# Ternary feedforward: the second quantisation moved to the middle of a VectorE step, the bias matmuls ahead of its transposes, and one ScalarE eviction between the two activations

## The reference

```python
def act_quant(x):
    scale = 127.0 / jnp.clip(jnp.max(jnp.abs(x), axis=-1, keepdims=True), 1e-05)
    q = jnp.clip(jnp.round(x * scale), -128.0, 127.0) / scale
...
def bitlinear158(x, w, b):
    xq = act_quant(rms_norm(x))
    wq = weight_quant(w)
    return jnp.einsum('bsd,od->bso', xq, wq) + b
...
h = jax.nn.silu(bitlinear158(x, w1, b1))
h = jax.nn.gelu(h, approximate=False)
h = layer_norm(h, ln_g, ln_b)
return bitlinear158(h, w2, b2)
...
x = _layernorm(x + _L1_ffn_ref(x, ...), axis=-1)
```

## Time and profile before

| | us |
|---|---|
| median of 3 runs | 2614.13 |
| lowest and highest | 2604.57, 2614.92 |
| the profiled execution, its own time | 2613.25 |
| its span, first to last instruction | 2611.5 |

### The profile page before, as it was taken

One profiled execution on the slowest core, in us unless ns is written; L12 is line 12 of the kernel. 1 busy time (PEld: TensorE's weight loads), 2 busy tenths in 40 slices (PEclk: granted clock), 3 DMA queues, 4 the chain that ended last, 5 costly groups with the idle time before them and its releaser, 6 DMA issues. The chain is left out here.

```text
span 2611.5 us, 32892 instructions
## 1 busy us (share of the span) xinstructions
PE 1969.5 (75%) x11984; PEld 1450.6 (56%) x11984; DVE 1357.5 (52%) x2704; ACT 741.0 (28%) x1233; POOL 450.7 (17%) x470
## 2 busy tenths in 40 slices
PE   3258888323665999999999995999968996267766
PEld 2135555222434777777877784787846774133333
DVE  8657766486554232222322314566554776456666
ACT  1015555100211221121121112222214002565565
POOL 0122321000000000000000001010103765023334
PEclk9859998656876999999999997999988998588887
DMA  4099995312534000000000003000013114500000
GB/s 177 21 139 153 145 158 85 113 36 83 175 112 162 1 17 18 1 17 18 1 17 17 9 1 113 17 33 17 17 44 137 43 41 152 202 8 25 24 17 24
DMA packets 111911, 169.17 MB, mean 65 GB/s; under 512 B 9104, under 2 KB 65040, under 8 KB 109328
## 3 DMA queue, kind: packets, MB, share of 16 engines
q1 hardware_dynamic: 102672, 150.35, 23.2%
q10 hardware_dynamic: 9088, 16.78, 1.7%
HBM read 120.70 MB, written 46.14 MB: 64 GB/s over the span
## 5 line engine op out<-in xcount | busy, mean ns | idle before, releaser
L1317 DVE TENSOR_TENSOR f_hid<-f_gate,f_gu 128x256 f32<-128x256 f32 x264 | 111.1, 421 | 437.5 <-ACT f_gate L1229 434.3
L1229 ACT ACTIVATE f_gate<-f_gu 128x256 f32<-128x256 f32 x264 | 100.6, 383 | 485.9 <-PE f_gu L1140 352.1
L453 DVE TENSOR_REDUCE a_rowmax<-a_ring 128x2 f32<-128x512 f32 x256 | 165.0, 687 | 100.6 <-PE a_ring L532 98.5
L1974 PE MATMUL e_py<-e_kv,e_toep 128*128 128x320 f32 x640 | 179.1, 435 | 0.0
L1152 PE MATMUL f_gu<-f_low,f_bg 128*128 128x256 f32 x704 | 168.1, 380 | 6.5 <-DVE f_hid L1317 6.5
L1166 PE MATMUL f_pout<-f_wd,f_hid 128*128 128x512 f32 x352 | 165.4, 592 | 0.0
L1140 PE MATMUL f_gu<-f_xhi,f_wg 128*128 128x256 f32 x704 | 152.1, 314 | 4.1 <-issue 4.1
L405 ACT ACTIVATE a_prob<-a_sT 128x1024 f32<-128x1024 f32 x128 | 130.6, 1026 | 81.8 <-PE a_sT L521 81.7
L1974 PEld LDWEIGHTS e_py<-e_kv,e_toep 128*128 128x128 f32 x640 | 119.2, 190 | 45.7
L1152 PEld LDWEIGHTS f_gu<-f_low,f_bg 128*128 128x128 f32 x704 | 127.9, 190 | 28.4 <-issue 10.5
L1140 PE MATMUL f_gu<-f_xhi,f_wu 128*128 128x256 f32 x704 | 133.4, 288 | 0.0
(11 more groups left out here) (348 smaller groups left out, 4416.1 us busy)
## 6 DMA issues: line engine op xcount, KB each, us to landing
a_qs<-parts SPq DMA_DIRECT2D x96, 128.0 KB, 6.6
a_ks<-parts SPq DMA_DIRECT2D x96, 128.0 KB, 7.0
parts<-a_hi SPq DMA_DIRECT2D x16, 512.0 KB, 8.7
parts<-a_lo SPq DMA_DIRECT2D x16, 512.0 KB, 8.7
e_toep<-in_taps SPq DMA_DIRECT2D x32, 256.0 KB
a_xf<-in_xT SPq DMA_DIRECT2D x1, 4096.0 KB, 21.1
ctxT<-a_turned SPq DMA_DIRECT2D x16, 256.0 KB, 9.6
a_cf<-ctxT SPq DMA_DIRECT2D x1, 4096.0 KB, 13.1
```

Source lines behind the costliest of these rows:

```text
L453: dve.tensor_reduce(rowmax[:, s % 2, :, e * SLOTS + j], ring[n % RING][:, :].rearrange("p (q t) -> p q t", t=T), AX.X, ALU.max, negate=Tru ...
L1229: act.activation(gate[:, (u * H + n) % 2, :], gu[f % 4][:, 0, :], ACT.Silu).then_inc(gate_ready, 1)
L1317: dve.tensor_tensor(hid[:, f % 4, j, :], gate[:, (u * H + n) % 2, :], gu[f % 4][:, 1, :], ALU.mult).then_inc(hid_ready, 1)
L1974: last = pe.matmul(py[n % RING][:, 0:DIAG * BS], toep[:, h % 3, (t - j) * P:(t - j + 1) * P], kv[:, h % 2, j, :], start=(j == 0), stop=(j ...
```

## The change

Three orders inside a step change; no instruction is added or taken away, and no shape, buffer or wait changes.

- VectorE: the second quantisation (lag 5) goes from before L2339 to behind the tail's L2349, and the input's largest magnitude (L2353, lag 0) goes from behind the tail to ahead of it.
- TensorE: the bias matmuls (L2264, with their wait for `silu_done`) go from behind the transposes L2253 to ahead of them.
- ScalarE: the eviction `q1f` (L2208) goes from ahead of both activations to between the first and the second.

```diff
@@ -2202,15 +2202,15 @@
                         act.wait_ge(s_["mean_ready"], t + 1)
                         act.activation(junk[:, 0, :], ha[:, t % 3, :], ACT.Square, bias=hs[:, t, 1:2],
                                        accum_out=hs[:, t, 2:3]).then_inc(s_["var1"], 1)
-                    t = tile_at(s, 1)
-                    if t is not None:
-                        act.wait_ge(s_["q1_turned"], t + 1)
-                        act.activation(q1f[:, t % 2, :, :], pq1[:, :].rearrange("p (k t) -> p k t", k=KT), ACT.Identity,
-                                       bias=minus[:, :]).then_inc(s_["q1f_ready"], 1)
-                    for lag in ((2, 3) if s % 2 == 0 else (3, 2)):
+                    for first, lag in ((True, 2), (False, 3)) if s % 2 == 0 else ((True, 3), (False, 2)):
                         t = tile_at(s, lag)
                         if t is not None:
                             silu(t) if lag == 2 else gelu(t)
+                        t = tile_at(s, 1) if first else None
+                        if t is not None:
+                            act.wait_ge(s_["q1_turned"], t + 1)
+                            act.activation(q1f[:, t % 2, :, :], pq1[:, :].rearrange("p (k t) -> p k t", k=KT), ACT.Identity,
+                                           bias=minus[:, :]).then_inc(s_["q1f_ready"], 1)
                     t = tile_at(s, 0)
                     if t is not None:
                         act.wait_ge(got_x[t % XT], 16 * (t // XT + 1))
@@ -2242,6 +2242,16 @@
                         for j in range(KT):
                             last = pe.transpose(pq1[:, j * P:(j + 1) * P], xq[:, t % 2, j * P:(j + 1) * P], keep["ident"][:, :])
                         last.then_inc(s_["q1_turned"], 1)
+                    t = tile_at(s, 1)
+                    if t is not None:
+                        pe.wait_ge(s_["diag_ready"], t + 1)
+                        if t >= 1:
+                            pe.wait_ge(s_["silu_done"], t)
+                        else:
+                            pe.wait_ge(s_["w_ready"], KT)
+                        for n in range(QB):
+                            pe.matmul(p1[:, n * 512:(n + 1) * 512], diag[:, t % 2, :], b1[:, n * 512:(n + 1) * 512],
+                                      start=True, stop=False)
                     t = tile_at(s, 5)
                     if t is not None:
                         pe.wait_ge(s_["q2_ready"], t + 1)
@@ -2255,14 +2265,6 @@
                             last.then_inc(s_["q2_turned"], 1)
                     t = tile_at(s, 1)
                     if t is not None:
-                        pe.wait_ge(s_["diag_ready"], t + 1)
-                        if t >= 1:
-                            pe.wait_ge(s_["silu_done"], t)
-                        else:
-                            pe.wait_ge(s_["w_ready"], KT)
-                        for n in range(QB):
-                            pe.matmul(p1[:, n * 512:(n + 1) * 512], diag[:, t % 2, :], b1[:, n * 512:(n + 1) * 512],
-                                      start=True, stop=False)
                         pe.wait_ge(s_["q1f_ready"], t + 1)
                         for n in range(QB):
                             for j in range(KT):
@@ -2324,13 +2326,6 @@
                         xs.step(dve.tensor_scalar(row[:, 8:9], row[:, 5:6], wfac[:, :], None, ALU.mult))
                         dve.tensor_scalar(diag[:, t % 2, :], keep["ident"][:, :], row[:, 8:9], None, ALU.mult
                                           ).then_inc(s_["diag_ready"], 1)
-                    t = tile_at(s, 5)
-                    if t is not None:
-                        row, y = row2[:, t, :], hc[:, t % 2, :]
-                        dve.wait_ge(s_["root2"], t + 1)
-                        dve.wait_ge(s_["max2"], t + 1)
-                        scales(ys, row, 1)
-                        dve.tensor_scalar(y, y, row[:, 7:8], ROUND, ALU.mult, ALU.add).then_inc(s_["q2_ready"], 1)
                     t = tile_at(s, 4)
                     if t is not None:
                         dve.wait_ge(s_["var1"], t + 1)
@@ -2338,6 +2333,13 @@
                             dve.wait_ge(s_["q2_turned"], (t - 1) * KT)
                         dve.scalar_tensor_tensor(hc[:, t % 2, :], ha[:, t % 3, :], hs[:, t, 1:2], gain[:, :], ALU.add, ALU.mult
                                                  ).then_inc(s_["gained"], 1)
+                    t = tile_at(s, 0)
+                    if t is not None:
+                        dve.wait_ge(got_x[t % XT], 16 * (t // XT + 1))
+                        dve.tensor_reduce(row1[:, t, 3:4], xt[:, t % XT, :], AX.X, ALU.max, apply_absolute_value=True
+                                          ).then_inc(s_["max1"], 1)
+                        if t == 1:
+                            ternary(1)
                     t = tile_at(s, 6)
                     if t is not None:
                         x = xt[:, t % XT, :]
@@ -2347,13 +2349,13 @@
                         dve.wait_ge(s_["added"], t + 1)
                         tails.step(dve.bn_stats(stats[:, t, 0:6], x))
                         dve.bn_aggr(stats[:, t, 6:8], stats[:, t, 0:6]).then_inc(s_["var_ready"], 1)
-                    t = tile_at(s, 0)
+                    t = tile_at(s, 5)
                     if t is not None:
-                        dve.wait_ge(got_x[t % XT], 16 * (t // XT + 1))
-                        dve.tensor_reduce(row1[:, t, 3:4], xt[:, t % XT, :], AX.X, ALU.max, apply_absolute_value=True
-                                          ).then_inc(s_["max1"], 1)
-                        if t == 1:
-                            ternary(1)
+                        row, y = row2[:, t, :], hc[:, t % 2, :]
+                        dve.wait_ge(s_["root2"], t + 1)
+                        dve.wait_ge(s_["max2"], t + 1)
+                        scales(ys, row, 1)
+                        dve.tensor_scalar(y, y, row[:, 7:8], ROUND, ALU.mult, ALU.add).then_inc(s_["q2_ready"], 1)
                     t = tile_at(s, 4)
                     if t is not None:
                         y = hc[:, t % 2, :]
```

## The result

| | before | changed |
|---|---|---|
| median, us (4 runs each) | 2611.04 | 2569.43 |
| lowest, highest | 2604.57, 2614.92 | 2568.12, 2572.93 |
| profiled execution, its span | 2611.5 | 2568.5 |
| last stage in it, first weight load to the end | 395.0 | 361.5 |

The account below looks back on a forecast made before the run. TensorE and ScalarE, waiting for each other in a 20.5 us loop per step, bound the kernel. Terms -42.9, -7.1, -5.1 and +11.7 net -43.4: 2569.9 from the profiled 2613.25, 2570.7 against the median, said 2571; range 2556 to 2588.

Parts of the forecast that it names:

- ten periods: Between the first and eleventh `w2` products: five odd-even pairs of 32.5 us, 162.5 against 205.4, 42.9 less.
- the eleventh: The eleventh period between `w2` products, 20.17 us before, becomes an even step without the magnitude, 13.1: 7.1 less.
- fill: From first `w1` to first `w2` product, 68.4 us before: four first steps together 5.1 shorter, `q1f` no longer delaying the activation.
- The ring: TensorE and ScalarE waiting for each other in a closed chain, 20.5 us a step, VectorE no part; the change opens it.
- An odd step, 18.8 us: Transposes 0.45, TensorE idle 3.95 until SiLU ends, slow-clock bias 5.22, transposes and evictions 2.3, products 6.9.
- The bound I gave above it: Whole odd-step bias at the low clock, 7.0 us instead of 5.22: 8.9 us more in all, kernel 2580.
- An even step, 13.7 us: Bias at full clock; VectorE's second quantisation ends last, transposes begin 4.5 us after `w2`, then 2.3 and 6.9.
- a sign of being wrong: Prediction counts as wrong if TensorE waits for VectorE's rounding in the middle steps too, not only the last four.
- The drain: Last four periods, input tiles gone: moved quantisation uncovered behind the tail; 11.9, 14.4, 14.4, 11.5, together 52.2 against 40.55, 11.7 lost.
- The clock did not hold through the wait: Rival: clock stays up through odd steps' 3.95 us idle; odd steps 17.1, kernel 2562 or less; chance 0.17.
- VectorE did not become the bound of the middle steps: Rival: VectorE and ScalarE bound every step, even steps at 15.0 instead of 13.7; kernel 2580 to 2590; chance 0.14.
- the dearer rivals: VectorE and ScalarE bounding every step (0.14), or TensorE at low clock all odd step, 10.6 more each, 2624 (0.05).

Follow-up runs that it names:

- two second traces: The kernel of before and the changed kernel each traced once more with no edit; last stage 396.2 and 359.8 us.
- x5_fill: Changed kernel plus four f32 matmuls with unused results between the input's transposes and the bias in odd steps; 2561.0 us, ratio to before 0.9803.
- x1_dve_old: Changed kernel with VectorE's order put back to that of before, TensorE and ScalarE keeping the new orders; 2553.7 us, ratio to before 0.978.

## Why the prediction came out right, and where it was off

The forecast of 2571 against 2569.4 is closer than its steps, and that closeness is luck. Against the stage's own rows:

| term | predicted, us | first trace, us |
|---|---|---|
| ten periods | -42.9 | -35.7 |
| the eleventh | -7.1 | -6.7 |
| fill | -5.1 | -4.8 |
| last four periods | +11.7 | +14.0 |
| rest of the stage | 0 | -0.2 |
| ahead of the stage | 0 | -9.6 |
| sum | -43.4 | -43.0 |

Two terms of the sum, the ten periods and the last four, were mis-sized by 9.5 us together, and the stage's earlier start by 9.6 us, for which the prediction had no term, made good for it. In stage time the forecast was -43.4 and the measurement -33.4 and -36.4. The fill agrees in the first trace; in the two second traces the difference is 7.5.

**The ring.** Right, and shown from both sides: undoing TensorE's or ScalarE's order brings its length back in part, each alone opens it in part, both together open it. The waits changed as said: in the middle steps TensorE's wait for `q2f` fell from 6.3 to 0.4.

**An odd step, 18.8 us.** It measured 20.15. The failing term is the bias: 5.22 was taken from a row of the fill with the same idle time of 4.15 us, and it is 6.15. The window of the kernel before over that idle time says why the row was not the same case:

```profile
2275.50:2279.40 3.90, 0.00 (x0) 0.03 (x1) 0.00 (x0) 3.87 (x4) 0.00 (x0) 0.50 0.00 0
```

There the clock was low through the whole wait and rose within the bias; in an odd step of the changed kernel it falls only within the wait, and more of the low stretch is left for the bias. Of the 1.35 us, 0.93 are this, 0.2 the idle time (4.15 instead of 3.95) and 0.2 the transposes. The bound I gave above it, 7.0 with the whole bias at the low level, holds it. The five odd steps make 5.9 of the 7.2 us by which the ten periods were off (the first is 19.37, with a bias of 5.37), the even ones the other 1.3.

**An even step, 13.7 us.** It measured 13.97. Its size was right, its limit named wrongly: I had VectorE's rounding end last. With the quantisation early again the period is 13.9, and the chain runs over `q1f`, table load, GELU, squares and `q2f` on ScalarE. VectorE's part was real (TensorE does wait up to 0.5 us for the rounding there), but with it gone the ring over ScalarE is only 0.1 us shorter. By the letter of the prediction this wait in middle steps was also a sign of being wrong, though its own sum for the even step had 0.55 us of it.

**The drain.** The mechanism was right: no bias covers the moved quantisation. The four were 52.2 in the sum and 54.5 in the trace. The second and third agree (14.1, 14.2 for 14.4, 14.4); the first is 12.9 for 11.9, the larger part of it since VectorE's scale and shift (L2362, in the changed kernel L2364) ahead of it takes 3.37 us instead of 2.35, and the last 13.2 for 11.5, of which 1.7 is a `w2` product at the low clock level (5.18), which I had put at 3.45 though a row of the old drain had one at 5.94. TensorE's waits for the rounding there are 3.8 to 4.6 us, where I had said 4 to 7.

**The rivals.** The clock did not hold through the wait, as `x5_fill` shows by what it gives when it does: 11.5 us over ten periods, where the rival had 8.6. VectorE did not become the bound of the middle steps (`x1_dve_old`), and TensorE was back at the full level before the transposes of the odd step (the third window above), so neither of the dearer rivals came. The switch of tables costs 1.30 us in the changed kernel too (2473.29 to 2474.59 in the chain). The 2.66 us that the Trainium skill ("ScalarE: Activation LUTs", "What ACT_TABLE_LOAD costs") gives for a switch do not show in this chain, in which every other piece has its row.

**What the prediction did not ask.** It weighed the three orders as one. Taken apart, VectorE's has no net gain in any combination: it adds 12.5 to 13.7 us to the stage of before, 13.3 to TensorE's order, 2.8 to ScalarE's, and 16 to 17 to both. Beside ScalarE's order alone it does shorten the ten periods (194.3 to 186.1) and gives more than that back in the last four (40.5 to 54.5). Its cost in the drain stood in the sum as +11.7; that leaving it out would save that much was one line further.

## What to carry to other kernels

In a pipeline of in-order engines, cost each moved piece by itself, and lay the drain and fill out as well as the middle: a piece moved behind work that covers it in the middle stands uncovered where that work has run out. A wait of TensorE costs more than its own length when the clock falls in it; here filler matmuls of 3.5 us in a wait of 4.15 took 2.5 us off a step. And where a change lies in one of several stages, measure that stage from its first instruction, since here the unchanged part moved the total by up to 12.5 us.

## What the runs showed of the hardware

A shorter wait cost more than a longer one. In the variant with TensorE's order alone the bias ran after 6.04 us of idle and, a step later, after 2.73:

```profile
2433.51 5.34 PE L2253 MATMUL g_p<-g_b,g_diag 128*128 128x512 f32 x8 [6.04 <-ACT g_ha L2193]
...
2451.43 3.67 PE L2253 MATMUL g_p<-g_b,g_diag 128*128 128x512 f32 x8 [2.73 <-ACT g_ha L2193]
```

After 6.04 us it took 5.2 (5.34 less the overlap with the transposes), after the changed kernel's 4.15 us 6.15, and after 4.15 us in the fill of before 5.22. The windows of that variant ahead of the slow bias and over it (columns as above):

```profile
2427.40:2433.50 6.10, 0.07 (x1) 0.02 (x1) 6.00 (x7) 5.96 (x6) 1.80 (x3) 0.72 0.00 0
2433.50:2438.70 5.20, 5.19 (x9) 2.20 (x10) 3.48 (x10) 0.48 (x2) 2.24 (x3) 0.68 0.22 62
```

With two levels, 1.00 and 0.50, a mean of 0.72 over 6.10 us is 3.4 us at the low one (2 x 0.28 x 6.10), spent idle, and 0.68 over the bias another 3.3. In the changed kernel it is 1.8 us of the idle 4.10 (mean 0.78) and 5.0 of the bias (0.55 over 5.5). So here the idle time ahead of the bias did not tell its price; the longer wait took more of the low stretch upon itself.

An instruction of GpSimd and one of VectorE took 1.0 us longer each when they met in the changed kernel's drain:

```profile
2494.72 1.29 DVE L2358 TENSOR_SCALAR g_hc<-g_hc,g_row 128x2048 f32<-128x2048 f32 x1
2494.88 2.26 POOL L2162 TENSOR_TENSOR g_xt<-g_xt,g_b 128x512 f32<-128x512 f32 x1
2495.92 3.37 DVE L2364 SCALAR_TENSOR_TENSOR g_hc<-g_hc,g_hs,g_shift 128x2048 f32<-128x2048 f32 x1
```

GpSimd's 128x512 addition takes 1.27 us in the middle steps and VectorE's L2364 2.35. There the addition comes later in the step, behind the root of the input's squares, and lies beside VectorE's `TENSOR_REDUCE` (2.29 us), where neither is longer; in the drain that root is missing, and it begins 1.04 us before L2364. The rows fit one waiting for the other rather than both running slower: the addition ends 1.13 us after the rounding ahead of it (2497.14 against 2496.01), and L2364 ends 2.15 us after the addition (2499.29). A middle step has the like, a 128x1 instruction of GpSimd that takes 0.19 us elsewhere in the step and here ends with VectorE's `gained`:

```profile
2469.84 2.35 DVE L2334 SCALAR_TENSOR_TENSOR g_hc<-g_ha,g_hs,g_gain 128x2048 f32<-128x2048 f32 x1 [0.66 <-ACT g_junk L2203]
2469.89 2.35 POOL L2138 TENSOR_SCALAR g_hs<-g_hs 128x1 f32<-128x1 f32 x1 [1.12 <-ACT g_junk L2203]
```

No run moved one of these instructions by itself, so the cause is not shown.
